# First keys of a sequence taken inside the last feed-forward turns, and two blocks of scores moved ahead of key tiles 3 and 4

## The chip, the cores and the metric

The kernel runs on one NeuronCore of a Trainium2 chip. Its engines are TensorE (PE, matrix products), VectorE (DVE), ScalarE (ACT), GpSimd (POOL) and SyncE (SP, which issues the transfers here). They run side by side and meet at semaphores. The metric is device time in microseconds (us): the median of several runs.

## The reference

The input x is 2 sequences of 4096 rows of 256 numbers. Three layers follow each other: a feed-forward layer, a causal attention, and the same feed-forward layer again.

```
x = x + 0.5 * ffn(layernorm(x))          # mix over 3 rows, 9 paths, argmax picks one, layernorm
x = x + attention(layernorm(x))
x = x + 0.5 * ffn(layernorm(x))

# attention(x):
q, k, v = x @ Wq.T + bq, x @ Wk.T + bk, x @ Wv.T + bv
scores  = q @ k.T / 16
masked  = where(causal, scores * sign(scores), -inf)    # the absolute value of the score
out     = softmax(masked) @ v
return out @ Wo.T + bo
```

## The kernel before, in words

**Tiles.** A tile is 512 rows (4 blocks of 128). There are 16 tiles, 8 per sequence. All products run in three fp16 matmuls (high x high, high x low, low x high), so most data exist as a high part, made by ACT, and a low part, made by DVE.

**Feed-forward (`ffn(0)`, `ffn(1)`).** Each engine goes through turns -6 to 16, and in turn t works on several tiles at different stages. At the end of a tile stand `result` (DVE adds the path's product to the row, and counts `y_done`), `squares` (ACT), `result_scale` (POOL, the reciprocal root), `result_scaled` and `result_added` (DVE), and a store by SP, which counts `stored`. The product of tile 15 goes to its own PSUM banks 6 and 7. While turns 11 to 15 run, the first five tiles of x1 (the result of the first layer) are loaded back, and DVE and POOL work out their means and deviations (`first_stats`, `first_scales`).

**Attention (`attention(b)`, b = 0 and 1).** W_q and W_k are folded into one matrix and W_v and W_o into another, so the normalised rows serve as keys and as values. For each key tile t:
- `key_rows(t)` (ACT or DVE) normalises the rows in place,
- `keys(t, c)` (PE) transposes them into two PSUM banks,
- `keyT_high` (ACT) and `keyT_low` (DVE; `key_lows` is both halves) make the fp16 parts of the transposed keys,
- `key_high` (ACT) and `key_low` (POOL) make those of the rows as values.

`query(j, c)` (PE) makes the queries of tile j, `q_high` (ACT) and `q_low` (DVE) their parts. `group((j, m))` is a block of scores of query tile j against key tile m: PE makes four strips, ACT takes the absolute value (`absolute`) and DVE the running maximum (`score_max`). Key tiles 0 to 4 and the blocks (0, 0) and (1, 0) are made before the steps; then `step(j)`, j = 0 to 7, does the rest. A step opens with a transpose of the running maximum (PE, L1878), a reduce on DVE (L1139) and a transpose back (PE, L1887), from which ACT makes `max_row`. DVE subtracts it from the scores (L1041), ACT takes the exponential and its high part (L1458, L1462), DVE the low part (L1047), and PE multiplies with the values.

**What sets the order.** Nothing schedules this program: every engine runs its instructions in the order in which its block is written, and waits where the code says so. Waits that matter here: before sequence 0 PE waits for `y_done` of all 16 tiles; `keys_wait(t)` on PE waits for the low part of key tile t; `query(j, c)` and the first block of scores of a query tile wait for `spare_free[c]`, which `q_low` and the two users of banks 6 and 7 at a step's opening count; a block of scores waits until ACT has emptied the same strip of the block before it (`abs_done`); POOL's `key_low` before sequence 0 waits for `x1_done` of all 16 tiles; SP loads key tile 5 when all 16 tiles are stored. Between the sequences, key tiles 0 to 2 and queries 0 and 1 of the next sequence are made inside step 7 of the one before; key tiles 3 and 4 are made after it, together with the four outputs of the last tile.

Of the kernel before, what the change touches and what calls it, by code (L numbers as in the profile page):

```python
# [49 lines left out]
def macaron(nc, x, Wq, bq, Wk, bk, Wv, bv, Wo, bo, mix, W1, b1, W2, b2, Wo1, bo1, Wo2, bo2,  # L50
# [11 lines left out]
    with ctx:  # L62
# [208 lines left out]
        def key_bank(t):  # L271
            return 4 if t % 2 == 0 else 0
# [60 lines left out]
        def use(ph, t):  # L333

            return ph * NTT + t
# [35 lines left out]
        def out_banks(t):  # L371

            return ps_n if t == NTT - 1 else ps_o

# [295 lines left out]
        def _(dve):  # L670
# [140 lines left out]

            def ffn(ph):
# [33 lines left out]

                def result_scaled(t):

                    dve.wait_ge(r_rstd, use(ph, t) + 1)
                    for u in range(SUB):  # L850
                        at = cols(n_rows(t), u * D, D)
                        ins = v.scalar_tensor_tensor(out=at, in0=at, scalar=y_rstd[:, u:u + 1], in1=gamma_b[:, :],  # L852
                                                     op0=ALU.mult, op1=ALU.mult)
                    ins.then_inc(scaled_done, 1)

                def result_added(t):

                    dve.wait_ge(xb_done, use(ph, t) + 1)
                    dve.wait_ge(scaled_done, use(ph, t) + 1)
                    v.tensor_tensor(n_rows(t), n_rows(t), x_rows(t), ALU.add).then_inc(x1_done, 1)  # L860
# [52 lines left out]
                def turn(t):  # L913
# [45 lines left out]
                    if last:  # L959
                        result_scaled(t - 1)  # L960
# [4 lines left out]
                    if last:  # L965
                        result_added(t - 1)
                        if ph == 0 and 0 <= t - 1 - NT < EARLY:
                            added_sums(t - 1)
# [8 lines left out]
            def attention(b):  # L977
# [225 lines left out]
                if b == 0:  # L1203
                    for t in range(EARLY - 1):
                        key_lows(t)
                        if t in (1, 2):
                            for c in range(DC):
                                q_low(t - 1, c)
                        if t < 2:
                            key_rows(EARLY - 2 + t)  # L1210
                    group(one_by_one(0, 0, True), None, lambda i: None)
                    key_lows(EARLY - 1)
                else:
# [5 lines left out]
                    output(s_last, 1)  # L1219
                    for c in range(DC):  # L1220
                        keyT_low(AHEAD_KEYS, c, LATE_BANK)
                    score_max(*maxima[2])
                    output(s_last, 2)
                    score_max(*maxima[3])
                    output(s_last, 3)
                    key_rows(AHEAD_KEYS + 1)
# [19 lines left out]
        def _(act):  # L1246
# [42 lines left out]

            def ffn(ph):  # L1290
# [27 lines left out]

                def squares(t):
                    g = use(ph, t)  # L1320
                    act.wait_ge(y_done, g + 1)
                    if g >= 1:
                        act.wait_ge(r_eps, g)
                    for u in range(SUB):
                        ins = a.activation(cols(square, u * D, D), cols(n_rows(t), u * D, D), ACT.Square, accum_out=y_sq[:, u:u + 1])  # L1325
                    ins.then_inc(sq_done, 1)
# [37 lines left out]
                def turn(t):  # L1364
# [9 lines left out]
                    if last:  # L1374
                        squares(t - 1)
# [19 lines left out]
            def attention(b):  # L1395
# [172 lines left out]
                if b == 0:  # L1568
                    key_rows(0)
                    keysT_high(0)  # L1570
                    key_rows(1)
                    keysT_high(1)
                    key_rows(2)

                    act.wait_ge(stored, 16 * (NTT - 2))
                    for j in range(2):
                        for c in range(DC):
                            q_high(j, c)
                        keysT_high(j + 2)
                        key_high(j)  # L1580
                    group(None, (0, 0, True), None, lambda i: None)
                    absolute(SUB - 1, True, blocks(act, b, 0, 0), ring_at(act, 0, 0))
                    keysT_high(EARLY - 1)
                    for t in range(2, EARLY):
                        key_high(t)
# [429 lines left out]
```

## Time and profile before

| | |
|---|---|
| runs | 1462.21, 1463.25, 1463.43 us, median 1463.25 |
| profiled execution, from first to last instruction | 1460.0 us |
| PE busy | 1336.2 us (92%) |
| DVE busy | 1178.4 us (81%) |
| ACT busy | 923.2 us (63%) |
| POOL busy | 326.0 us (22%) |
| mean granted clock of TensorE | 0.977 |

The profiled execution is told by its span alone; the median of the runs is 3.25 us above it. `ffn(0)` fills the first 320 us, sequence 0 goes to about 750 us, sequence 1 to about 1190 us, and `ffn(1)` fills the rest. A busy share is a mean over all of these; the change touches two short stretches, the passage from `ffn(0)` to sequence 0 (about 300 to 350 us) and the one from sequence 0 to sequence 1 (about 750 to 785 us), and those have to be looked at by themselves.

### The profile page before, as it was taken

The numbers are of one execution on the slowest core, as the hardware profiler recorded it, in microseconds if no ns is written. First come the engines' busy times: TensorE is split into PE (matmuls) and PEld (weight loads), VectorE is DVE, ScalarE is ACT, GpSimd is POOL, SyncE is SP. The second block draws the span as 40 slices with busy tenths as digits, with TensorE's granted clock in tenths as the row PEclk, the third lists the DMA queues.
The fourth block names the chain that finished last, engine by engine and source line by source line (L and its number), as shares of the span: only waits on it lengthen the run. The fifth ranks groups of instructions, "written<-read, shape, count | busy, mean of one in ns | idle before, by whom it ended". The sixth has DMA issues, their size and how long they took to land.

```text
span 1460.0 us, 24657 instructions
## 1 busy us (share of the span) xinstructions
PE 1336.2 (92%) x7700; PEld 773.8 (53%) x7700; DVE 1178.4 (81%) x2326; ACT 923.2 (63%) x1717; POOL 326.0 (22%) x359
## 2 busy tenths in 40 slices
PE   3999998868999999999879999999998879999995
PEld 2567765644454454544344455454544336777764
DVE  5999998876778777788875787787778768989986
ACT  5676764446567666566866567666575866766641
POOL 2255553432010000040011010000130004555422
PEclk9899999979999999999999999999999989999998
DMA  6243333320001100011201010000002211433321
GB/s 157 51 125 109 113 99 91 92 73 0 16 29 36 38 0 29 1 44 38 79 1 44 30 44 16 29 15 15 29 15 74 86 32 51 121 93 108 92 79 58
DMA packets 86985, 82.18 MB, mean 56 GB/s; under 512 B 8539, under 2 KB 86884, under 8 KB 86884
## 3 DMA queue, kind: packets, MB, share of 16 engines
q1 hardware_dynamic: 86884, 80.91, 18.4%
q8 instruction: 54, 0.88, 0.3%
q14 instruction: 47, 0.39, 0.1%
HBM read 55.43 MB, written 25.46 MB: 55 GB/s over the span
## 4 chain that ended last, share of the span: by engine, by line
PE 64%; DVE 15%; issue 9%; ACT 8%; POOL 2%; DMA 1%; DVEq 0%; ACTq 0%; POOLq 0%; SPq 0%
PE PS L1618 57%; DVE R L1047 2%; PE PS L1626 2%; DVE R L1041 2%; PE PS L1716 2%; ACT R L1458 2%; ACT R L1462 2%; DVE run_max L1035 1%; PE PS L1687 1%; DVE x_st L1069 1%; ACT R L1417 1%; POOL R L608 1%; DVE R L852 1%; DVE st L751 1%; DMA R<-in_L_attn_x 1%
## 5 line engine op out<-in xcount | busy, mean ns | idle before, releaser
L1618 PE MATMUL PS<-R 128*128 128x512 f16 (+3 forms) x3456 | 718.4, 362 | 36.1 <-DVE R L1047 29.7
L1618 PEld LDWEIGHTS PS<-R 128*128 128x128 f16 (+1 forms) x3456 | 325.9, 98 | 395.6 <-DVE R L1047 58.8
L1047 DVE TENSOR_TENSOR R<-R 128x512 f16<-128x512 f32 (+3 forms) x288 | 188.7, 655 | 96.1 <-ACT R L1462 94.4
L1449 ACT ACTIVATE R<-PS 128x512 f32 (+5 forms) x288 | 160.3, 558 | 158.8 <-PE PS L1618 158.8
L1458 ACT ACTIVATE R<-R 128x512 f32<-128x512 f32 (+4 forms) x288 | 169.6, 589 | 52.2 <-DVE R L1041 51.3
L1618 PE MATMUL PS<-R,w_hi 128*128 128x512 f16 x640 | 195.5, 388 | 4.3 <-DVE R L801 4.3
L1618 PE MATMUL PS<-w_hi,R 128*128 128x256 f16 x1024 | 189.0, 274 | 10.5 <-DVE R L843 10.5
L1462 ACT ACTIVATE R<-R 128x512 f16<-128x512 f32 (+3 forms) x288 | 171.1, 594 | 26.7 <-ACT R L1458 0.4
L1041 DVE TENSOR_TENSOR R<-R,max_row 128x512 f32<-128x512 f32 (+4 forms) x288 | 186.8, 648 | 0.5 <-ACT max_row L1526 0.5
L1035 DVE TENSOR_TENSOR run_max<-run_max,R 128x512 f32<-128x512 f32 (+3 forms) x272 | 175.6, 645 | 8.4 <-DVE run_max L1035 1.7
L575 POOL TENSOR_SCALAR veps<-mv 128x4 f32<-128x4 f32 x48 | 16.4, 343 | 653.4 <-issue 376.0
L1618 PE MATMUL PS<-w_lo,R 128*128 128x256 f16 x512 | 140.2, 274 | 0.0
L904 DVE SCALAR_TENSOR_TENSOR R<-PS,b1c,R 128x512 f32<-128x512 f32 x128 | 93.4, 742 | 38.3 <-PE PS L1618 37.5
L1618 PE MATMUL PS<-R,w_lo 128*128 128x512 f16 x320 | 123.8, 387 | 0.0
L1618 PEld LDWEIGHTS PS<-w_hi,R 128*128 128x128 f16 x1024 | 100.6, 98 | 37.6 <-DVE R L843 13.4
L640 POOL TENSOR_TENSOR R<-R 128x1024 f16<-128x1024 f32 x16 | 34.2, 2154 | 308.6 <-ACT R L1424 308.6
L1626 PE MATMUL PS<-ident,R 128*128 128x128 f32 x384 | 58.6, 298 | 39.7 <-ACT R L1266 18.8
L1325 ACT ACTIVATE R<-R 128x256 bf16<-128x256 f32 x128 | 51.6, 404 | 61.9 <-DVE R L843 61.9
L1618 PEld LDWEIGHTS PS<-R,w_hi 128*128 128x128 f16 x640 | 60.9, 103 | 52.3 <-issue 4.7
L910 DVE TENSOR_TENSOR R<-R 128x1024 f16<-128x1024 f32 x64 | 77.7, 1214 | 0.0
L1272 ACT ACTIVATE R<-PS 128x1024 f32<-128x1024 f32 x32 | 32.8, 1025 | 69.6 <-PE PS L1626 69.5
L608 POOL TENSOR_TENSOR R<-R,beta_b 128x1024 f32<-128x1024 f32 x32 | 75.3, 2354 | 4.9 <-DVE R L901 4.7
(124 smaller groups left out, 1752.5 us busy)
## 6 DMA issues: line engine op xcount, KB each, us to landing
R<-x_scratch SPq DMA_DIRECT2D x48, 512.0 KB, 4.1
x_scratch<-R SPq DMA_DIRECT2D x32, 512.0 KB, 3.2
R<-oh_scratch SPq DMA_DIRECT2D x32, 320.0 KB
R<-in_L_attn_x SPq DMA_DIRECT2D x16, 512.0 KB, 5.1
R<-oh_scratch SPq DMA_DIRECT2D x32, 256.0 KB
out<-R SPq DMA_DIRECT2D x16, 512.0 KB, 3.2
R<-in_L_ffn_W SPq DMA_DIRECT2D x2, 288.0 KB
R<-in_L_ffn_W SPq DMA_DIRECT2D x1, 512.0 KB
```

The costliest lines, as they stand in the source:

```text
L608: g.tensor_tensor(rows4(x_rows(t)), rows4(x_rows(t)), beta_b[:, :].unsqueeze(1).to_broadcast([P, SUB, D]), ALU.add).then_inc(xb_done, 1)
L904: v.scalar_tensor_tensor(out=at, in0=ps_h[:, h_bank[g, c], :], scalar=b1c[:, c:c + 1], in1=chunk(mask, t, c), op0=ALU.add, op1=ALU.mult).t ...
L910: v.tensor_tensor(chunk(hlo, t, c, n), masked_chunk(t, c, n), chunk(hhi, t, c, n), ALU.subtract)\
L1035: v.tensor_tensor(run_max[:, lo:], run_max[:, lo:], cols(ring, at, TT - lo), ALU.max)\
L1041: v.tensor_tensor(cols(ring, at, TT - lo), cols(ring, at, TT - lo), max_row[:, lo:], ALU.subtract)\
L1047: v.tensor_tensor(p_lo[:, i * TT + lo:(i + 1) * TT], pf[:, (i % 2) * TT + lo:(i % 2 + 1) * TT], p_hi[:, i * TT + lo:(i + 1) * TT], ALU.sub ...
L1325: ins = a.activation(cols(square, u * D, D), cols(n_rows(t), u * D, D), ACT.Square, accum_out=y_sq[:, u:u + 1])
L1449: a.activation(cols(ring, ring_m + i * TT + lo, TT - lo), ps_s[:, i, lo:], ACT.Abs, scale=1.0 / (QS * XS * D ** 0.5)).then_inc(abs_done, 1)
L1458: a.activation(p, cols(ring, ring_n + i * TT + lo, TT - lo), ACT.Exp)\
L1462: a.activation(p_hi[:, i * TT + lo:(i + 1) * TT], p, ACT.Copy).then_inc(phi_done, 1)
L1618: ins = t_.matmul(dst, w, xx, start=start and n == 0, stop=stop and n == last, skip_group_check=skip)
L1626: ins = t_.transpose(dst[:, u * P:(u + 1) * P], cols(rows, u * D + c * P, P), ident[:, :])
```

## The change

Passage 1, `ffn(0)` to sequence 0:
- PE waits for `y_done` of 15 tiles only, transposes key tiles 0 and 1, and then waits for tile 15. Key tile 1 goes to banks 0 and 1, the others to banks 4 and 5. Block (0, 0) follows query 1 at once and no longer waits for key tile 2's low part; block (1, 0) stands between key tiles 3 and 4.
- ACT normalises key tiles 0 and 1 inside turn 15 and key tile 2 after the high parts of 0 and 1. `squares` of tile 15 moves behind the high part of key tile 2.
- DVE does `result_scaled` and `result_added` of tiles 14 and 15 between the low parts, and the maxima of block (0, 0) before the low part of key tile 3.

Passage 2, sequence 0 to sequence 1: block (1, 0) stands before key tiles 3 and 4 on PE, with outputs 2 and 3 inside it; ACT and DVE follow.

```diff
         def key_bank(t):
-            return 4 if t % 2 == 0 else 0
+            return 0 if t == 1 else 4
...
+        def left_over(ph, t):
+
+            return ph == 0 and t >= NTT - 2
...
-                    if last:
-                        result_scaled(t - 1)
+                    if last and not left_over(ph, t - 1):
+                        result_scaled(ph, t - 1)
```

On DVE, before sequence 0:

```diff
                 if b == 0:
-                    for t in range(EARLY - 1):
-                        key_lows(t)
-                        if t in (1, 2):
-                            for c in range(DC):
-                                q_low(t - 1, c)
-                        if t < 2:
-                            key_rows(EARLY - 2 + t)
+                    key_lows(0)
+                    key_lows(1)
+                    result_scaled(0, NTT - 2)
+                    for c in range(DC):
+                        q_low(0, c)
+                    key_lows(2)
+                    key_rows(3)
+                    result_added(0, NTT - 2)
+                    for c in range(DC):
+                        q_low(1, c)
+                    key_rows(4)
+                    result_scaled(0, NTT - 1)
                     group(one_by_one(0, 0, True), None, lambda i: None)
-                    key_lows(EARLY - 1)
+                    result_added(0, NTT - 1)
+                    key_lows(3)
+                    key_lows(4)
```

On ACT, in the turn:

```diff
+                    if ph == 0 and t == NTT - 1:
+                        first_key_rows(0)
+                        first_key_rows(1)
```

On PE, before sequence 0 and, under `else`, before sequence 1:

```diff
                 if b == 0:
-                    pe.wait_ge(y_done, NTT)
-                    for t in range(EARLY - 1):
...
+                    pe.wait_ge(y_done, NTT - 1)
+                    for t in range(2):
                         for c in range(DC):
                             keys(t, c, key_bank(t))
...
+                    pe.wait_ge(y_done, NTT)
...
                 else:
+                    def late_outputs(i):
+                        if i == 1:
+                            for u in range(2, SUB):
+                                output(b * NT - 1, b * SPARE + 2, u)
+
                     keys_wait(AHEAD_KEYS - 1)
                     group((0, 0, True), None, lambda i: None)
                     for u in range(2):
                         output(b * NT - 1, b * SPARE + 2, u)
+                    group((1, 0, False), None, late_outputs)
                     for c in range(DC):
                         keys(AHEAD_KEYS, c, LATE_BANK)
-                    for u in range(2, SUB):
-                        output(b * NT - 1, b * SPARE + 2, u)
                     keys_wait(AHEAD_KEYS)
                     for c in range(DC):
                         keys(AHEAD_KEYS + 1, c, LATE_BANK)
-                group((1, 0, False), None, lambda i: None)
```

The order of PE's instructions at the end of passage 1, before: the rows are key tile 3 (transposes), block (0, 0) in four rows, key tile 4, block (1, 0) and the opening of step 0.

```order
L1626 MATMUL PS<-ident,R 128x128 x8
L1618 MATMUL PS<-R 128x512 x6
L1618 MATMUL PS<-R 128x384 x6
L1618 MATMUL PS<-R 128x256 x6
L1618 MATMUL PS<-R 128x128 x6
L1626 MATMUL PS<-ident,R 128x128 x8
L1618 MATMUL PS<-R 128x512 x24
L1878 MATMUL PS<-ident,run_max 128x128 x4
```

And now, PE at the same place of the changed kernel, from block (0, 0) on:

```order
L1641 MATMUL PS<-R 128x512 x6
L1641 MATMUL PS<-R 128x384 x6
L1641 MATMUL PS<-R 128x256 x6
L1641 MATMUL PS<-R 128x128 x6
L1649 MATMUL PS<-ident,R 128x128 x8
L1641 MATMUL PS<-R 128x512 x24
L1649 MATMUL PS<-ident,R 128x128 x8
L1901 MATMUL PS<-ident,run_max 128x128 x4
```

Block (0, 0) stands ahead of key tile 3 and block (1, 0) ahead of key tile 4, whose transposes are now the last thing before step 0.

DVE in passage 1, before, from `result` of tile 14 (L843) on; L852 is `result_scaled`, L860 `result_added`, L1007 a low part of keys, L995 `key_rows`.

```order
L843 SCALAR_TENSOR_TENSOR R<-PS,R 128x1024
L751 BN_STATS st<-R 128x6 x4
L758 BN_AGGR mv<-st 128x2 x4
L852 SCALAR_TENSOR_TENSOR R<-R,y_rstd,gamma_b 128x256 x4
L860 TENSOR_TENSOR R<-R 128x1024
L843 SCALAR_TENSOR_TENSOR R<-PS,R 128x1024
L852 SCALAR_TENSOR_TENSOR R<-R,y_rstd,gamma_b 128x256 x4
L860 TENSOR_TENSOR R<-R 128x1024
L1007 TENSOR_TENSOR R<-PS,R 128x512 x2
L995 TENSOR_SCALAR R<-R,key_rstd,key_shift 128x256 x4
```

And now, DVE from `result` of tile 14 (L862) on; L821 is `result_scaled`, L829 `result_added`, L1011 a low part of keys, L1022 one of a query, L999 `key_rows`.

```order
L862 SCALAR_TENSOR_TENSOR R<-PS,R 128x1024
L755 BN_STATS st<-R 128x6 x4
L762 BN_AGGR mv<-st 128x2 x4
L862 SCALAR_TENSOR_TENSOR R<-PS,R 128x1024
L1011 TENSOR_TENSOR R<-PS,R 128x512 x4
L821 SCALAR_TENSOR_TENSOR R<-R,y_rstd,gamma_b 128x256 x4
L1022 SCALAR_TENSOR_TENSOR R<-PS,R 128x512 x2
L1011 TENSOR_TENSOR R<-PS,R 128x512 x2
L999 TENSOR_SCALAR R<-R,key_rstd,key_shift 128x256 x4
L829 TENSOR_TENSOR R<-R 128x1024
L1022 SCALAR_TENSOR_TENSOR R<-PS,R 128x512 x2
```

`result` of tile 15 follows that of tile 14 with only the statistics between them, and the scaling and adding of both tiles comes later, between the key and query parts.

PE in passage 2, before: the last output row, key tile 4, block (1, 0) and the opening of step 0.

```order
L1618 MATMUL PS<-wvo_lo,R 128x257
L1618 MATMUL PS<-wvo_hi,R 128x257
L1626 MATMUL PS<-ident,R 128x128 x8
L1618 MATMUL PS<-R 128x512 x24
L1878 MATMUL PS<-ident,run_max 128x128 x4
```

And now, PE at the same place: outputs 2 and 3 end in the first two rows, the second half of block (1, 0) follows, then key tiles 3 and 4.

```order
L1641 MATMUL PS<-wvo_lo,R 128x257
L1641 MATMUL PS<-wvo_hi,R 128x257
L1641 MATMUL PS<-R 128x512 x12
L1649 MATMUL PS<-ident,R 128x128 x16
L1901 MATMUL PS<-ident,run_max 128x128 x4
```

No product is added or dropped on PE; the two key tiles moved behind the block of scores.

## Rows read from the trace of the kernel before

**Rows 1.** Waits of PE, whole span: who waited, for whom, us, times, longest

```profile
PE PS L1626 <- ACT R L1417: 13.6, 2, 10.9
PE PS L1626 <- DVE R L995: 6.2, 1, 6.2
```

**Rows 2.** Windows, passage 1: busy time of each engine, granted clock, DMA

```profile
305.00:310.00 5.00, 0.00 (x0) 0.00 (x0) 4.60 (x5) 0.00 (x0) 4.65 (x6) 0.85 0.00 0
310.00:315.00 5.00, 0.00 (x0) 0.00 (x0) 1.84 (x3) 3.45 (x12) 2.04 (x5) 0.50 0.31 105
```

**Rows 3.** Timeline of PE, passage 1: start, us, instruction, idle before it and releaser

```profile
315.37 1.94 PE L1626 MATMUL PS<-ident,R 128*128 128x128 f32 x8 [10.89 <-ACT R L1417]
...
327.10 0.59 PE L1618 MATMUL PS<-R,wqk_hi 128*128 128x512 f16 x2
...
329.69 1.04 PE L1626 MATMUL PS<-ident,R 128*128 128x128 f32 x8
332.68 3.43 PE L1618 MATMUL PS<-R 128*128 128x512 f16 x24 [1.95 <-DVE R L1007]
335.95 1.04 PE L1626 MATMUL PS<-ident,R 128*128 128x128 f32 x8
336.83 5.34 PE L1618 MATMUL PS<-R 128*128 128x512 f16 x24
342.01 0.60 PE L1878 MATMUL PS<-ident,run_max 128*128 128x128 f32 x4
```

**Rows 4.** Timeline of DVE, passage 1

```profile
300.92 1.22 DVE L843 SCALAR_TENSOR_TENSOR R<-PS,R 128x1024 f32<-128x1024 f32 x1
...
314.68 1.67 DVE L852 SCALAR_TENSOR_TENSOR R<-R,y_rstd,gamma_b 128x256 f32<-128x256 f32 x4 [3.16 <-POOL y_rstd L598]
316.46 1.22 DVE L860 TENSOR_TENSOR R<-R 128x1024 f32<-128x1024 f32 x1
...
334.82 0.29 DVE L1028 TENSOR_TENSOR R<-R,tri 128x128 f32<-128x128 f32 x1 [2.19 <-ACT R L1449]
...
337.68 1.28 DVE L1007 TENSOR_TENSOR R<-PS,R 128x512 f16<-128x512 f32 x2
...
343.25 2.03 DVE L1032 COPY run_max<-R 128x512 f32<-128x512 f32 x1
...
350.17 0.68 DVE L1041 TENSOR_TENSOR R<-R,max_row 128x512 f32<-128x512 f32 x1
```

**Rows 5.** Timeline of ACT, passage 1

```profile
313.16 2.06 ACT L1417 ACTIVATE R<-R,key_shift,key_rstd 128x256 f32<-128x256 f32 x4
...
336.59 1.09 ACT L1430 ACTIVATE R<-PS 128x512 f16<-128x512 f32 x2 [0.16 <-PE PS L1626]
337.56 2.95 ACT L1424 ACTIVATE R<-R 128x1024 f16<-128x1024 f32 x3
```

**Rows 6.** Timeline of POOL, passages 1 and 2

```profile
338.70 6.30 POOL L640 TENSOR_TENSOR R<-R 128x1024 f16<-128x1024 f32 x3 [4.09 <-ACT R L1424]
...
756.45 4.25 POOL L640 TENSOR_TENSOR R<-R 128x1024 f16<-128x1024 f32 x2 [115.82 <-ACT R L1424]
```

**Rows 7.** Timeline of PE, passage 2

```profile
764.13 1.94 PE L1626 MATMUL PS<-ident,R 128*128 128x128 f32 x8 [6.25 <-DVE R L995]
765.87 7.03 PE L1618 MATMUL PS<-R 128*128 128x512 f16 x24
...
774.46 0.60 PE L1887 MATMUL PS<-ident,max_col 128*128 128x128 f32 x4
```

**Rows 8.** Timeline of DVE, passage 2

```profile
758.09 0.64 DVE L1028 TENSOR_TENSOR R<-R,tri 128x128 f32<-128x128 f32 x1
758.76 2.23 DVE L1035 TENSOR_TENSOR run_max<-run_max,R 128x256 f32<-128x256 f32 x1
...
767.35 1.39 DVE L1069 BATCH_NORM_STATS2 x_st<-R 128x6 f32<-128x256 f32 x4
...
780.89 0.68 DVE L1041 TENSOR_TENSOR R<-R,max_row 128x512 f32<-128x512 f32 x1
```

More of the change, by code:

```diff
@@ L810, in set_beginnings, with result_scaled, result_added @@
                 v.memset(chunk(mask, 1, 0)[0:DM, :], 0.0).then_inc(edges_set, 1)
+            def result_scaled(ph, t):
+                dve.wait_ge(r_rstd, use(ph, t) + 1)
+                for u in range(SUB):
+                    at = cols(n_rows(t), u * D, D)
+                    ins = v.scalar_tensor_tensor(out=at, in0=at, scalar=y_rstd[:, u:u + 1], in1=gamma_b[:, :],
+                                                 op0=ALU.mult, op1=ALU.mult)
+                ins.then_inc(scaled_done, 1)
+            def result_added(ph, t):
+                dve.wait_ge(xb_done, use(ph, t) + 1)
+                dve.wait_ge(scaled_done, use(ph, t) + 1)
+                v.tensor_tensor(n_rows(t), n_rows(t), x_rows(t), ALU.add).then_inc(x1_done, 1)
             def ffn(ph):
@@ L845, in result @@
                         .then_inc(y_done, 1)
[L847 to L860, printed above, removed]
                 def added_sums(t):
@@ L964, in turn @@
                             masked_low(t + HIDDEN, 2)
-                    if last:
-                        result_added(t - 1)
+                    if last and not left_over(ph, t - 1):
+                        result_added(ph, t - 1)
                         if ph == 0 and 0 <= t - 1 - NT < EARLY:
@@ L1219, in attention @@
                     output(s_last, 1)
+                    score_max(*maxima[2])
+                    score_max(*maxima[3])
+                    key_rows(AHEAD_KEYS + 1)
+                    output(s_last, 2)
+                    output(s_last, 3)
                     for c in range(DC):
                         keyT_low(AHEAD_KEYS, c, LATE_BANK)
[L1222 to L1226, printed above, removed]
                     for c in range(DC):
@@ L1288, in x_high, with squares, first_key_rows @@
                 a.activation(cols(xhi, g % XBUF * DC * TT, DC * TT), xm, ACT.Copy).then_inc(xhi_done, 1)
+            def squares(ph, t):
+                g = use(ph, t)
+                act.wait_ge(y_done, g + 1)
+                if g >= 1:
+                    act.wait_ge(r_eps, g)
+                for u in range(SUB):
+                    ins = a.activation(cols(square, u * D, D), cols(n_rows(t), u * D, D), ACT.Square, accum_out=y_sq[:, u:u + 1])
+                ins.then_inc(sq_done, 1)
+            def first_key_rows(t):
+                act.wait_ge(f_scaled, t + 1)
+                act.wait_ge(f_in[t], 16)
+                for u in range(SUB):
+                    at = cols(rows_in[t], u * D, D)
+                    ins = a.activation(at, at, ACT.Identity, bias=key_shift[:, t, u:u + 1], scale=key_rstd[:, t, u:u + 1])
+                ins.then_inc(a_rows[t], 1)
             def ffn(ph):
@@ L1373, in turn @@
                         middle(ph, t + MIX)
-                    if last:
-                        squares(t - 1)
+                    if ph == 0 and t == NTT - 1:
+                        first_key_rows(0)
+                        first_key_rows(1)
+                    if last and not (ph == 0 and t == NTT):
+                        squares(ph, t - 1)
                     if rows_on(ph, t + ROWS):
@@ L1592, in attention @@
                     key_high(0)
+                    group(None, (1, 0, False), None, lambda i: None)
                     keysT_late(AHEAD_KEYS)
@@ L1595, in attention @@
                     keysT_late(AHEAD_KEYS + 1)
-                    for t in range(2, EARLY):
-                        key_high(t)
-                group(None, (1, 0, False), None, lambda i: None)
+                for t in range(2, EARLY):
+                    key_high(t)
                 over_steps(act, step)
```

58 lines of the change are left out of this document (28 added, 30 removed).

## The prediction, made before the changed kernel was run

> **What bounds the kernel now.** I read the waits of PE first, because PE is busy 92% of the span and everything else hides behind it. Two of its waits belong to the passages that the change touches: 13.6 us for ACT's L1417, in two pieces, and 6.2 us for DVE's L995 in one [rows 1]. Then I read the windows of passage 1. Between 305 and 315 us PE does nothing, and the granted clock falls to 0.50, which is 1.2 GHz; it is back at 2.4 GHz only when PE has worked again for some us [rows 2]. Last come the timelines, engine by engine, to see who holds whom. In passage 1 PE stands idle for 10.9 us before it transposes key tile 0 at 315.37, so it ended tile 15's product at about 304.5 [rows 3]. It waits because ACT normalises the rows of key tile 0 only at 313.16 [rows 5], after `squares` of tile 15, which waits for DVE's `result` of tile 15, which stands on DVE behind the scaling of tile 14. In passage 2 PE waits 6.25 us for the rows of key tile 4, and the block of scores that follows it takes 7.03 us for the work that took 5.2 in passage 1 [rows 7, 3], because the clock fell in that gap.
>
> **Passage 1, step by step.** Prices of PE's pieces at 2.4 GHz, as distances between starts in [rows 3]: a key tile 336.83 - 335.95 = 0.9, a pair of queries 329.69 - 327.10 = 2.6, block (0, 0) 335.95 - 332.68 = 3.3, block (1, 0) 342.01 - 336.83 = 5.2 us. From the start of a key tile to the end of its second low part I build 2.4 us: 0.65 until ACT starts on the first half (336.59 - 335.95, [rows 3, 5]), 1.1 for ACT's two copies [rows 5], 0.6 for the last low part, and small gaps.
>
> *Front.* ACT is free from about 294 and normalises key tiles 0 and 1 there, 2 x 2.06 us [rows 5]; nothing waits behind them but `squares` of tile 14, whose input comes at 302.1 (300.92 + 1.22, [rows 4]). Cost nothing, cover 4 us. PE then goes from tile 15's product (304.4) straight into key tiles 0 and 1, until 306.1. DVE makes `result` of tile 15 at 304.5 to 305.7, key lows 0 at 305.7 to 306.9 and 1 until 308.2 (0.6 us each, two in 1.28 in [rows 4]). PE: queries 0 at 306.95 to 309.55 (waiting 0.85), key tile 2 to 310.4, queries 1 to 313.05, block (0, 0) to 316.35, key tile 3 to 317.25, block (1, 0) to 322.45. ACT has 2.06 us of key rows 2 in between and is done with them at 309.2, in time.
>
> *DVE becomes the longer queue.* After key lows 1 (308.2) it runs: scaling of 14, 1.65 (start 314.68, [rows 4]), query lows 0, 1.2 (to 311.0), key lows 2, 1.2 (to 312.2), key rows 3, 1.35, adding of 14, 1.15 (start 316.46, [rows 4]), query lows 1, 1.2 (to 316.0), key rows 4, 1.35, scaling of 15, 1.65, the maxima of (0, 0), 337.68 - 334.82 = 2.9, adding of 15, 1.15 (to 323.0), key lows 3, 1.2: 324.2. The price of key rows is that of four 128x256 operations at 0.33; no row shown has it, and the four scalings bound it from above with 1.65. PE waits for key lows 3 from 322.45 to 324.3, makes key tile 4 until 325.2 and opens step 0 (L1878) there instead of at 342.01: 16.8 us earlier. DVE must still make key lows 4 (to 326.8) and the reduce (to 327.4), so the transpose back starts at 327.4. Before it came 1.7 us after L1878, at 343.7: **16.3 us earlier**. The clock never falls here, since PE's gaps are 0.85 and 1.85 us, where before the mean of 0.85 in the window from 305 puts the fall at about 308.5, after 4 us without work [rows 2].
>
> *What is late next.* `x1_done` of 16 tiles now comes at 323.0, so POOL makes its five `key_low` of 2.1 us each (6.30 for three, [rows 6]) from 323.0 until 333.6 or later (ACT's last three high parts, 2.95 us from 326.05 [rows 5], are in time for it). Before, they ended at 345.0, that is 3.0 us after L1878; now 8.4 us after it. They matter for what they take from DVE, not for what they make. The copy of the first maximum at 343.25 took 2.03 us because it ended only with POOL's last operation, and in passage 2 a small operation took 0.64 us and the next, 128x256, 2.23 us beside two of POOL's [rows 4, 6, 8]: the two take turns, one operation each. DVE's operations that read PSUM ran beside POOL undelayed. After the reduce DVE has a copy and three maxima to make from SBUF, and each lets one `key_low` through: POOL's work of 10.6 us from 323.0 plus three such turns of 0.45 ends at about 335.0, the last maximum at 335.2. Then come the two query lows (1.2) and L1041 at **336.4**; it stood at 350.17. That is 13.8 us, against 16.3 with no such delay; I take 13.7. The whole chain behind L1041 (exponential, high part, low part, values on PE) keeps its length. The bounds are 16.3 (POOL yields, or runs ahead) and 11.5 (every DVE operation here takes the 2.23 us of [rows 8]: 5 x 2.23 from 327.4 ends 3 us later than I have it, less 0.8 of overlap).
>
> [...]
>
> *The store and the loads behind it.* Tile 15 is stored some 5 us later than before, at about 326, and SP's loads of key tile 5 and of the first residual stand behind it, landing at about 331. DVE looks at tile 5 in a later step, tens of us on. Cost nothing.
>
> **Passage 2, step by step** (times as in the before trace, as if passage 1 had changed nothing). PE ends outputs 0 and 1 at 754.4. Then block (1, 0) with outputs 2 and 3 inside it, 5.2 + 1.3, to 760.85, key tile 3 to 761.75; its rows are ready, and those of tile 4 come at 759.6 at the latest, delayed by one `key_low`. ACT and DVE make the parts of key tile 3 until 763.3 (2.4 from the start of its transposes), PE key tile 4 at 763.35 to 764.2 and L1878 there. On DVE key lows 4 end at 765.75, then the four sums of the outputs, 1.39 us [rows 8], which were hidden before, end at 767.1, and the reduce at 767.8. The transpose back starts at 767.8 instead of 774.46 [rows 7]: **6.65 us earlier**. POOL's second `key_low` now waits for ACT's high part 1 (763.5), so three and a half of them lie beside the copy and the maxima; by the same turns the last maximum ends at 773.8 and L1041 starts at 775.0 instead of 780.89 [rows 8]: **5.9 us**. Bounds: 8.7, which is what L1878 gains (765.87 + 7.03 = 772.9 against 764.2, [rows 7]) if the sums cost nothing, and 3.5, if each of the DVE operations takes 2.23.
>
> **The sum.** 13.7 + 5.9 = 19.6 us of the profiled 1460.0, which is 1440.4. The median of the runs stood 3.25 above the profiled span, so the runs give **1443.7**. Nothing between the passages changes in work, and PE is the bound there, so the gain is carried to the end.
>
> **The rivals.**
> - *POOL costs nothing.* Its operations fall beside PSUM reads of DVE, or DVE is served first. For it: the order of arrivals is close. Against: [rows 8]. 16.3 + 6.65 = 22.95: 1440.3 us. Chance 0.2.
> - *The clock falls in the new gap.* While DVE is held up, PE has no work from about 332.4 to 336.4, 4.0 us; the same length of idleness brought the clock down before [rows 2, 3]. Then some 7 us run at 1.2 GHz, as the block of [rows 7] did, of which PE was working about half or more: 3.4 us lost. Against: the gap is only just that long. 16.2 gained: 1447 us. Chance 0.15.
> - *Only passage 1 pays, or DVE's queue is longer than summed.* In passage 2 DVE gets the sums and POOL at once and gives back what PE won: 13.7 gained, 1449.5 us. Much the same comes out if three of DVE's operations in passage 1 are stretched by POOL as in [rows 8], 1.8 us each, with none of it hidden. Chance 0.12.
> - *It does not do what it says.* PE still waits for tile 15 or for rows in place of its neighbours, and passage 1 gains only the 10.9 us of idleness less the new waits, about 8 us: 1455. Chance 0.03.
> - *Slower.* The clock falls before 310 us, since PE has several short waits there, and stays at 1.2 GHz through both passages. PE's work from 304.4 to L1878 is 5 x 0.9 + 2 x 2.6 + 3.3 + 5.2 = 18.2 us, at half the clock 36.4, ending at 341: gain 1 us. In passage 2, 9.6 us of work take 19.2 and end where they ended before: gain 0. With 3 us more lost in each following step the time is 1468. For it: [rows 2] show the clock low through such a passage. Against: it rose there as soon as PE worked without a break. It decides only if the clock is low for more than 30 us. Chance 0.03.
>
> **How the numbers follow.** The forecast has 0.47, with its own range of 1441.5 to 1446. With the rivals on either side, 1439 to 1450.5 leaves out the last two, the far end of the third and what lies below 1439: 2 in 10. A change within 0.2% (3 us) cannot be told from none in this kernel: faster by more than that needs under 1460.3, and only the slower rival and a little of the one before it miss this. Faster 0.94, same 0.03, slower 0.03.
>
> **What the profile will show.** If the steps are right: PE's first transposes of keys within 1 us of tile 15's product, at clock 1.00; no PE wait for key rows over 1 us in either passage; L1901 (the old L1878) at about 325; a PE wait for DVE's key lows 3 of 1 to 2 us; a copy or maximum on DVE of over 2 us between 327 and 336 beside POOL's `key_low`; in passage 2, a PE wait before L1910 of 1 to 2 us for DVE's reduce. The forecast is wrong if the clock is below 1.00 anywhere between 305 and 345, if the first L1045 of step 0 starts far from 336, or if a later step has a PE wait that was not there before.

## The result and the profile after

| | before | after |
|---|---|---|
| median of the runs | 1462.73 us (4 runs, 1461.53 to 1463.43) | 1444.58 us (4 runs, 1444.09 to 1445.54) |
| span of the profiled execution | 1460.0 us | 1442.5 us |
| PE busy | 1336.2 us | 1335.2 us |

The ratio is 0.9881, with a 95% interval of 0.987 to 0.9893. The forecast was 1443.7 us. PE works as long as before; what went is idleness and low clock in the two passages.

Where the gain is made can be read exactly, because each step opens with the same two PE instructions in both traces. The table takes the differences of their starts, and those of the first subtraction behind them (L1041 before, L1045 now), each against the same start ahead of the passage (`result` of tile 14 for passage 1, the first subtraction of step 7 for passage 2). The last column, the first subtraction of step 1, is the gain that is left one step later:

| gain in us at | opening of step 0 | transpose back | first subtraction | first subtraction of step 1 |
|---|---|---|---|---|
| passage 1, forecast | 16.8 | 16.3 | 13.7 | 13.7 |
| passage 1, measured | 17.06 | 16.45 | 13.75 | 13.57 |
| passage 2, forecast | 8.7 | 6.65 | 5.9 | 5.9 |
| passage 2, measured | 8.39 | 6.48 | 5.29 | 4.63 |

PE's timeline in passage 1 of the changed kernel (start, us, instruction, idle before it and releaser) answers to [rows 3]:

```profile
303.74 1.91 PE L1649 MATMUL PS<-ident,R 128*128 128x128 f32 x16
306.62 0.59 PE L1641 MATMUL PS<-R,wqk_hi 128*128 128x512 f16 x2 [0.97 <-DVE R L1011]
...
312.67 3.42 PE L1641 MATMUL PS<-R 128*128 128x512 f16 x24
315.93 1.04 PE L1649 MATMUL PS<-ident,R 128*128 128x128 f32 x8
316.80 5.34 PE L1641 MATMUL PS<-R 128*128 128x512 f16 x24
323.45 1.09 PE L1649 MATMUL PS<-ident,R 128*128 128x128 f32 x8 [1.31 <-DVE R L1011]
324.38 0.60 PE L1901 MATMUL PS<-ident,run_max 128*128 128x128 f32 x4
...
326.72 0.65 PE L1910 MATMUL PS<-ident,max_col 128*128 128x128 f32 x4 [0.44 <-DVE max_col L1143]
...
336.03 9.23 PE L1641 MATMUL PS<-R 128*128 128x512 f16 x39 [4.11 <-DVE R L1022]
```

The gap of 10.9 us is gone: 16 transposes follow tile 15's product without a pause. PE waits 0.97 us and 1.31 us for low parts of keys, as the forecast had it (0.85 and 1.85). Before, block (0, 0) waited 1.95 us for the low part of key tile 3 (at 332.68, [rows 3]); now it stands ahead of that tile and the wait is gone. The new and largest wait is the last one, 4.11 us for the query's low part.

DVE's timeline tells why; before, the copy took 2.03 us and the subtraction stood at 350.17 [rows 4]:

```profile
325.98 0.68 DVE L1143 TENSOR_REDUCE max_col<-PS 128x4 f32<-128x512 f32 x1
326.58 2.30 DVE L1036 COPY run_max<-R 128x512 f32<-128x512 f32 x1
328.98 5.75 DVE L1039 TENSOR_TENSOR run_max<-run_max,R 128x512 f32<-128x512 f32 x3
334.65 1.28 DVE L1022 SCALAR_TENSOR_TENSOR R<-PS,R 128x512 f16<-128x512 f32 x2
335.85 0.68 DVE L1045 TENSOR_TENSOR R<-R,max_row 128x512 f32<-128x512 f32 x1
```

POOL at that time, where it ended at 345.0 before [rows 6]:

```profile
322.28 11.11 POOL L644 TENSOR_TENSOR R<-R 128x1024 f16<-128x1024 f32 x5 [7.04 <-DVE R L829]
```

The copy and three maxima take 8.2 us, where pool_late, below, has 2.8 us for them without POOL beside them. POOL's five `key_low` run through the same time and are stretched too, from 10.6 to 11.1 us.

Windows of passage 1 after (busy time of PE, PEld, DVE, ACT, POOL, then the granted clock), where [rows 2] had a dead PE and a clock of 0.50 from 308.5 on:

```profile
330.00:335.00 5.00, 1.92 (x14) 0.84 (x12) 4.79 (x4) 1.47 (x3) 3.39 (x2) 1.00 0.00 0
335.00:340.00 5.00, 3.96 (x11) 1.25 (x12) 4.85 (x11) 2.92 (x7) 0.00 (x0) 0.66 0.00 0
```

The 17 us at 1.2 GHz are gone, but a new stretch of 3.4 us at that level begins at 335.7, at the end of the gap of 4.11 us.

Passage 2, PE and DVE after, against [rows 7, 8]:

```profile
749.34 1.09 PE L1649 MATMUL PS<-ident,R 128*128 128x128 f32 x8 [1.57 <-DVE R L1011]
750.27 0.60 PE L1901 MATMUL PS<-ident,run_max 128*128 128x128 f32 x4
...
753.91 0.65 PE L1910 MATMUL PS<-ident,max_col 128*128 128x128 f32 x4 [1.75 <-DVE max_col L1143]
...
761.72 2.09 PE L1641 MATMUL PS<-R 128*128 128x512 f16 x6 [2.60 <-DVE R L1022]
```

```profile
742.23 3.18 DVE L999 TENSOR_SCALAR R<-R,key_rstd,key_shift 128x256 f32<-128x256 f32 x4
...
751.87 1.40 DVE L1073 BATCH_NORM_STATS2 x_st<-R 128x6 f32<-128x256 f32 x4
753.19 0.67 DVE L1143 TENSOR_REDUCE max_col<-PS 128x4 f32<-128x512 f32 x1
753.78 0.78 DVE L1036 COPY run_max<-R 128x512 f32<-128x512 f32 x1
754.66 5.76 DVE L1039 TENSOR_TENSOR run_max<-run_max,R 128x512 f32<-128x512 f32 x3
```

The wait of 6.25 us for the rows of key tile 4 is gone. DVE normalises these rows (L999) earlier, in 3.18 us for four, one of them held beside a `key_low`. The sums of the outputs (L1073) and the reduce hold the transpose back for 1.75 us, and the maxima are stretched here as well. Behind the gap of 2.60 us the six matmuls take 2.09 us where they take 1.46 at the full clock.

### The profile page after: what moved, and what is told of

Read it like the earlier page. It is cut to its first block, busy times and chain, and to the rows that moved or that the text cites. A ratio compares the mean times of both kernels' runs of the same rounds, so it can differ in the third digit from the quotient of the medians.

```text
span 1442.5 us, 24659 instructions
## 1 busy us (share of the span) xinstructions
PE 1335.2 (93%) x7700; PEld 772.8 (54%) x7700; DVE 1181.9 (82%) x2326; ACT 922.6 (64%) x1717; POOL 328.1 (23%) x359
## 4 chain that ended last, share of the span: by engine, by line
PE 62%; DVE 17%; issue 9%; ACT 7%; POOL 2%; DMA 1%; DVEq 0%; ACTq 0%; POOLq 0%; SPq 0%
PE PS L1641 56%; DVE R L1051 2%; DVE R L1045 2%; PE PS L1739 2%; PE PS L1649 2%; DVE run_max L1039 2%; ACT R L1481 2%; ACT R L1485 1%; DVE x_st L1073 1%; PE PS L1710 1%; DMA R<-in_L_attn_x 1%; DVE R L821 1%; POOL R L612 1%; DVE R L908 1%; ACT R L1440 1%
## 5 line engine op out<-in xcount | busy, mean ns | idle before, releaser
L1641 PE MATMUL PS<-w_hi,R 128*128 128x256 f16 x1024 | 188.2, 273 | 10.9 <-DVE R L862 10.9
L1039 DVE TENSOR_TENSOR run_max<-run_max,R 128x512 f32<-128x512 f32 (+3 forms) x272 | 180.8, 665 | 8.4 <-DVE run_max L1039 1.7
L1045 DVE TENSOR_TENSOR R<-R,max_row 128x512 f32<-128x512 f32 (+4 forms) x288 | 186.9, 649 | 0.5 <-ACT max_row L1549 0.5
```

What stands on the lines that cost most here:

```text
L1039: v.tensor_tensor(run_max[:, lo:], run_max[:, lo:], cols(ring, at, TT - lo), ALU.max)\
L1045: v.tensor_tensor(cols(ring, at, TT - lo), cols(ring, at, TT - lo), max_row[:, lo:], ALU.subtract)\
L1641: ins = t_.matmul(dst, w, xx, start=start and n == 0, stop=stop and n == last, skip_group_check=skip)
```

## The experiments

Theory: the front of passage 1 and the score order of passage 2 make independent gains, and part of both is lost because POOL's `key_low` and VectorE's copy and maxima take turns. Rivals: the gain is all of one passage; POOL has nothing to do with the late subtraction; the order of scores makes the gain in passage 1 too. All gains below are read as in the table above, from one profile each; "back" is the transpose back, "kept" the gain at the first subtraction of step 1. Ahead of passage 1, where the edits change nothing that PE waits for, the profiled executions already stand from 1.8 us later to 1.25 us earlier than the one before, so a median tells less than these columns. Medians are of 4 or 5 runs (11 for p2_only), ratios against the kernel before on the same chip.

| kernel | median us | ratio (95%) | passage 1: back, subtraction, kept | passage 2: back, subtraction, kept |
|---|---|---|---|---|
| after_again | 1445.36 | 0.989 (0.9873, 0.9906) | 16.45, 13.76, 13.50 | 6.48, 5.28, 2.90 |
| p1_only | 1449.79 | 0.9911 (0.9897, 0.9924) | 16.46, 13.77, 13.53 | -0.24, -0.24, -0.23 |
| p2_only | 1458.72 | 0.9977 (0.9968, 0.9986) | -0.05, -0.05, -0.05 | 6.48, 5.29, 4.80 |
| pool_late | 1444.75 | 0.9874 (0.9859, 0.9889) | 16.46, 16.41, 15.26 | 6.49, 6.44, 5.29 |
| pool_memset | 1441.24 | 0.9852 (0.9837, 0.9867) | 16.46, 16.41, 16.41 | 6.48, 6.44, 6.44 |
| p1_tail_old | 1448.36 | 0.9903 (0.9888, 0.9918) | 17.24, 14.98, 12.07 | 6.48, 5.29, 5.29 |
| sums_late | 1448.24 | 0.9901 (0.9885, 0.9916) | 16.45, 13.75, 13.74 | 7.76, 3.96, 2.38 |
| pool_slots | 1441.9 | 0.9859 (0.9844, 0.9875) | 16.45, 16.40, 16.05 | 6.44, 6.39, 6.05 |
| slots_sums | 1440.44 | 0.985 (0.9837, 0.9864) | 16.45, 16.39, 16.05 | 7.76, 7.71, 7.36 |
| slots_sums_tail | 1441.66 | 0.9861 (0.9845, 0.9877) | 17.25, 17.24, 15.42 | 7.78, 7.73, 7.38 |

**p1_only.** The edit puts the old order back before sequence 1, on PE (and accordingly on DVE and ACT):

```diff
                     for u in range(2):
                         output(b * NT - 1, b * SPARE + 2, u)
-                    group((1, 0, False), None, late_outputs)
                     for c in range(DC):
                         keys(AHEAD_KEYS, c, LATE_BANK)
...
+                    group((1, 0, False), None, lambda i: None)
```

> Passage 1 as in the changed kernel, passage 2 as before. My theory: the two gains are independent, and passage 1 brings 16 us until the transpose back of step 0 and 13.5 to 14 us at the first L1045 behind it, because GpSimd's key_low operations hold VectorE's copy and maxima there; 13.5 us stay until passage 2, and the median is 1448.5 to 1450. Rival 1 (passage 1 is worth little by itself, the keys of passage 2 make up the rest): over 1452. Rival 2 (passage 2's new order costs in truth): under 1446.

1449.79 us, as the theory said. Passage 1's gain is the same to 0.04 us with and without passage 2's.

**p2_only.** The kernel before, with passage 2 changed:

```diff
                     for u in range(2):
                         output(b * NT - 1, b * SPARE + 2, u)
+                    group((1, 0, False), None, late_outputs)
```

> Passage 1 as before, passage 2 as in the changed kernel. My theory: 4.6 to 5.5 us faster than before, 1457 to 1458: 8.4 us at the opening of step 0 of sequence 1, 6.5 at the transpose back (the four sums of the outputs and the reduce stand in its way), 5.3 at the first L1045. Rival (the order of scores is worth the whole of PE's wait of 6.25 us and the low clock behind it): 8 us or more, under 1455.

The steps are the expected ones (8.4, 6.5, 5.3), but the median of 1458.72 is 0.7 us above the upper edge of what I expected, a gain of 3.65 us in place of 4.6 or more; the interval of the ratio reaches from 2.0 to 4.7 us. In its profile 1.1 us are lost at the passage to the last layer, which has nothing to do with the edit (below). The rival's 8 us are excluded.

**pool_late.** POOL is held back:

```diff
                 for t in range(EARLY):
+                    if t == 2:
+                        pool.wait_ge(max_done, b * BLOCKS + 3 * SUB)
                     key_low(t)
```

> The changed kernel, with GpSimd's key_low of tiles 2, 3 and 4 held back until the maxima of block (1, 1) are made. My theory, that GpSimd and VectorE take turns at operations from SBUF: VectorE's copy takes 0.4 us and three maxima 2.0 us instead of 2.3 and 5.75, the first L1045 comes 2.5 us earlier in passage 1 and 1.1 in passage 2, PE's gap of 4.1 us shrinks to 1.5, the clock no longer falls behind either passage (0.2 to 0.7 us each): 3 to 5 us faster than the changed kernel, 1439.5 to 1441.5. If the collisions only move into step 0's low parts, up to 2 us less of it each. Rival (PE waits there for ScalarE's query parts, and GpSimd has nothing to do with it): no change within 0.5 us.

The steps are the expected ones, the median is not. The copy and the maxima are short again, and so the subtraction comes only 0.05 us later than the transpose back allows, in place of 2.7 and 1.2 us. DVE in passage 1 of pool_late:

```profile
328.69 0.42 DVE L1038 COPY run_max<-R 128x512 f32<-128x512 f32 x1
329.21 2.28 DVE L1041 TENSOR_TENSOR run_max<-run_max,R 128x512 f32<-128x512 f32 x3
...
342.24 1.59 DVE L1053 TENSOR_TENSOR R<-R 128x128 f16<-128x128 f32 x1 [0.76 <-ACT R L1487]
...
346.62 1.57 DVE L1038 COPY run_max<-R 128x512 f32<-128x512 f32 x1
```

But 1.15 us of it are given back in each passage, where the three `key_low` meet the copy of step 1 (1.57 us). The low part of 1.59 us costs nothing: PE has work. PE's gap is 1.46 us and the clock does not fall behind either passage. But the median of 1444.75 is no better than the changed kernel's and so on the rival's number; what speaks against the rival is the subtraction, 2.66 and 1.15 us earlier than in the changed kernel. The profiled execution lost 2.3 us at the passage to the last layer and 1.6 ahead of passage 1 against the one before, places that the edit does not touch.

**pool_memset.** Three of POOL's five operations only write; the low parts of key tiles 2 to 4 as values are left out:

```diff
+                    if 2 <= t < EARLY:
+                        g.memset(cols(KV_lo, t * SUB * D, SUB * D), 0.0).then_inc(a_lo, 1)
+                        return
                     g.tensor_tensor(cols(KV_lo, t * SUB * D, SUB * D), rows_in[t], cols(KV_hi, t * SUB * D, SUB * D),
                                     ALU.subtract).then_inc(a_lo, 1)
```

> The changed kernel, with GpSimd's key_low of tiles 2, 3 and 4 replaced by a memset of the same cells, which leaves out the low parts of those values: GpSimd writes SBUF and reads nothing. My theory by the rule that only a read of GpSimd holds VectorE's two-input operations: the three maxima take 0.6 to 0.7 us each whatever the memsets take, and the gain is that of pool_late without moved collisions, 3.5 to 5 us, 1439.5 to 1441. The copy may still be held, since it has one input only and was held before. Rival 1 (any operation of GpSimd holds VectorE): the maxima are stretched by the length of a memset each. Rival 2 (GpSimd has nothing to do with it): no change.

1441.24 us; 16.41 and 6.44 us are kept whole. In passage 2 the maxima, of which the first lies wholly beside the third memset, take 2.28 us for three as when they are alone; the copy of passage 1 is held for the length of all three memsets. DVE and POOL in passage 1, then in passage 2:

```profile
328.14 2.87 DVE L1039 COPY run_max<-R 128x512 f32<-128x512 f32 x1
331.11 2.28 DVE L1042 TENSOR_TENSOR run_max<-run_max,R 128x512 f32<-128x512 f32 x3
```

```profile
327.99 2.73 POOL L645 MEMSET R<- 128x1024 f16 x3
...
750.83 3.06 POOL L645 MEMSET R<- 128x1024 f16 x3 [0.52 <-ACT R L1450]
```

The third of these memsets by itself:

```profile
752.72 1.18 POOL L645 MEMSET R<- 128x1024 f16 x1
```

```profile
752.48 0.52 DVE L1039 COPY run_max<-R 128x512 f32<-128x512 f32 x1
753.11 2.28 DVE L1042 TENSOR_TENSOR run_max<-run_max,R 128x512 f32<-128x512 f32 x3
```

So rival 2 is out, and rival 1 is out for the maxima, though on one overlap only: the first of them runs from 753.11 to 753.80, inside the memset of 752.72 to 753.90. The theory's price of POOL is settled: 2.7 us in passage 1 and 1.2 in passage 2 at the subtraction. The copy is the exception: even operations that only write hold it in passage 1. In passage 2 it took 0.52 us across the end of the second memset, and the third, which started under it, took 1.18 us where the others take 0.95.

**p1_tail_old.** The old order of scores with the new front (on PE; DVE makes the low part of key tile 3 before the scaling of tile 15, and ACT follows):

```diff
-                    group((0, 0, True), None, lambda i: None)
                     keys_wait(2)
                     for c in range(DC):
                         keys(3, c, key_bank(3))
-                    group((1, 0, False), None, lambda i: None)
+                    group((0, 0, True), None, lambda i: None)
                     keys_wait(3)
                     for c in range(DC):
                         keys(4, c, key_bank(4))
+                    group((1, 0, False), None, lambda i: None)
```

> The changed kernel, but in passage 1 the blocks of scores stand in the old order: key tile 3 before block (0, 0), key tile 4 before block (1, 0), low parts of key tile 3 before the scaling of tile 15. My theory: in passage 1 the front (keys 0 and 1 at once, late scaling and adding) makes nearly all of the gain, and the order of scores is worth under 1 us: the transpose back of step 0 within 1 us of the changed kernel's, the first L1045 0.5 to 1.5 us later since the last adding, and with it GpSimd's work, comes 1.2 us later; the median within 1.5 us of the changed kernel's. Rival (a block of scores hides a whole wait for the parts of a key tile): 3 us or more slower than the changed kernel.

The transpose back comes 0.8 us earlier, not later, than with the new order, and the subtraction 1.2 us earlier: my theory had the sign of the second wrong, because the shorter queue on DVE before the reduce outweighs POOL's later start. Of the 16.5 us none is thus due to the order of scores. But only 12.07 us are kept. Windows of passage 1 in this kernel:

```profile
335.00:340.00 5.00, 3.26 (x9) 0.99 (x8) 4.82 (x13) 3.68 (x8) 0.00 (x0) 0.52 0.00 0
340.00:345.00 5.00, 5.00 (x22) 2.33 (x21) 1.17 (x5) 1.22 (x4) 0.00 (x0) 0.79 0.00 0
```

The clock is at 1.2 GHz for 6.8 us from 335.2, where the changed kernel has 3.4. DVE, POOL and PE show a second cause of the 2.9 us that go between the subtraction and the next step:

```profile
334.01 1.41 DVE L1045 TENSOR_TENSOR R<-R,max_row 128x512 f32<-128x512 f32 x1
```

```profile
322.86 12.00 POOL L644 TENSOR_TENSOR R<-R 128x1024 f16<-128x1024 f32 x5 [8.25 <-DVE R L829]
```

```profile
337.64 9.49 PE L1641 MATMUL PS<-R 128*128 128x512 f16 x42 [1.74 <-DVE R L1051]
346.97 0.61 PE L1901 MATMUL PS<-ident,run_max 128*128 128x128 f32 x4
```

The subtraction meets POOL's last `key_low`, which ends at 334.86, and takes 1.41 us in place of 0.68: PE starts on the values 3.63 us after the subtraction's start instead of 2.91 (353.08 - 350.17 before). From there to the opening of step 1 it needs 9.33 us in place of 7.15. So 0.7 us are the collision and 2.2 the low clock; neither theory had them. The median of 1448.36 is 3.8 us above the first one of the changed kernel, which is the number of the rival; its mechanism is refuted by the transpose back, which lost nothing. The profiled execution took 1445.81 us, inside the expected range, and the other three 1448.33 to 1448.43: what these lost besides is not shown.

**sums_late.** The sums of the last output leave the place ahead of the reduce:

```diff
                         if is_int(j, 0) and i == SUB:
+                            if b:
+                                for u in range(SUB):
+                                    output_sums(s_last, u, xr)
...
-                    for u in range(SUB):
-                        output_sums(s_last, u, xr)
```

> The changed kernel, with the four sums of the last output moved behind the maxima of block (1, 0) in passage 2. My theory: the reduce and the transpose back come 1.3 us earlier in passage 2, but GpSimd's turns with the copy and the maxima end when they did, and the sums then stand before the query parts: the first L1045 of sequence 1 comes at most 0.3 us earlier, or up to 1.4 later. Median within 1.5 us of the changed kernel's. Rival (the transpose back sets the end): 1.3 us faster.

The steps are as expected: the transpose back gains 1.3 us, the subtraction loses 1.3, since the maxima take 5.76 us as before and the sums come on top. PE's gap grows to 5.21 us, the clock falls for 6.8 us, and the median is worse than I allowed for: its four runs (1447.49 to 1448.55) all lie above the eight of the changed kernel (1444.09 to 1446.39). This is the trap in a plain form: PE's visible wait before L1910 was not the one that set the end.

**pool_slots.** POOL's work placed in VectorE's idle time:

```diff
                 for t in range(EARLY):
+                    if t in (2, 4):
+                        pool.wait_ge(max_done, b * BLOCKS + (2 if t == 2 else 3) * SUB)
                     key_low(t)
```

> The changed kernel, with GpSimd's key_low of tiles 2 and 3 held back until the maxima of block (1, 0) are made, and that of tile 4 until those of block (1, 1). They then lie beside VectorE's idle time and its reads of PSUM. My theory: the 2.65 us at the first L1045 of passage 1 that pool_late won are kept but for some 0.4, and the copy of step 1, which pool_late stretched from 0.4 to 1.6 us, is short again: 3.5 to 4.5 us faster than the changed kernel, 1440 to 1441. Rival (each key_low costs VectorE the same wherever it stands): as pool_late, within 1 us of the changed kernel.

1441.9 us, 0.9 above the upper edge of what I expected. The subtraction is held by 0.3 us only (L1047, the subtraction here, takes 1.02 in place of 0.68), and 16.05 and 6.05 us are kept. The clock does not fall behind either passage. The rival is out: what a `key_low` costs depends on what it meets.

**slots_sums.** Both edits. 

> pool_slots and sums_late together. My theory: with GpSimd out of the way the sums fill VectorE's idle time between the maxima and the query parts, and the transpose back sets the time of passage 2: 1 to 1.3 us faster than pool_slots, 1439 to 1440. Rival (the sums are on no path in either): no change against pool_slots within 0.3 us.

1440.44 us, 0.4 above the expected range; 1.3 us more in passage 2, as expected, by the very edit that alone brought the subtraction 1.3 us later than in the changed kernel. It has the lowest median of the study.

**slots_sums_tail.** The same with the old order of scores in passage 1. 

> slots_sums with the tail of p1_tail_old: the old order of scores and key tiles in passage 1. My theory: the old order opened step 0 earlier (transpose back 17.24 us gained against 16.45) and lost it again only because GpSimd's work was later and PE's gap brought the clock down; with key_low of tiles 2 to 4 held back it keeps 16.6 to 17 us of passage 1, 0.6 to 0.9 us more than slots_sums: 1439.5 to 1440. Rival (the new order of scores is itself what keeps passage 1's gain): 1 us or more slower than slots_sums, over 1441.5.

The median is 1.2 us above slots_sums and so on the number that I had given the rival, but the two were not run on the same chip, and their runs overlap (1440.17 to 1442.27 against 1439.6 to 1441.21). My theory failed in one step, and the trace gives another cause than the rival's. 17.24 us are there at the subtraction's start, but 15.42 are kept. DVE and POOL in passage 1:

```profile
333.46 2.50 DVE L1047 TENSOR_TENSOR R<-R,max_row 128x512 f32<-128x512 f32 x1
```

```profile
324.58 4.41 POOL L644 TENSOR_TENSOR R<-R 128x1024 f16<-128x1024 f32 x2 [8.24 <-DVE R L831]
331.21 4.21 POOL L644 TENSOR_TENSOR R<-R 128x1024 f16<-128x1024 f32 x2 [2.22 <-DVE run_max L1041]
```

With the opening earlier, the subtraction falls into the second of the two `key_low` and takes 2.50 us. The shift of 0.8 us turned a collision of 0.3 us into one of 1.8; the passages together keep 22.8 us against 23.4 in slots_sums. Another 1.6 us of its profile went at the passage to the last layer. Whether the old order with a better place for that `key_low` would win was not tried.

**after_again.** 

> The changed kernel once more, beside slots_sums_tail on one chip, so that the two can be compared: 1444 to 1445.5. Its profile shows how much of the loss at the passage to the last layer (1.2 us in the first profile) is of the kernel: if it comes from where the clock falls, it differs between executions of one kernel.

1445.36 us. The steps repeat to 0.1 us up to the subtractions of step 0. What differs is the clock: in passage 2 it is low for 6.8 us in place of 3.4, and 2.90 us are kept in place of 4.63; at the passage to the last layer it is low for 10.2 us in place of 13.7, and nothing is lost against the one before, which has 10.2 us there too, in place of 1.2. Passage 2 stands in two other profiles with the same gain at the subtraction (5.29): p2_only, low for 3.4 us, kept 4.80, and p1_tail_old, where the clock stayed at 1.00 behind the same gap of 2.60 us, kept all of it.

## Why the prediction was right

*Front of passage 1: right.* ACT's early key rows cost nothing, and all starts of PE up to step 0 are within 0.3 us of the working once the 0.6 us that this execution had gained earlier are taken off. p1_tail_old shows that this front, not the order of scores, makes the gain.

*DVE becomes the longer queue: right.* The sum of thirteen prices missed the end of the queue by less than 0.3 us. PE's wait for key lows 3 was 1.31 us, where 1.85 were forecast.

*What is late next: right, and the term that mattered.* A sum that stopped at the transpose back would have had 22.95 us, and the rival that said so is refuted by pool_late and pool_memset, which get just these times when POOL is out of the way. The turns were forecast to put the subtraction at 336.4; it came at 335.85, at the same distance from the front. The lower bounds of 11.5 and 3.5 us counted five operations of 2.23 us where the queue has a copy and three maxima; the runs came nowhere near them. The Trainium skill (SBUF — State Buffer, "Who interferes with whom") states that a VectorE instruction with two SBUF inputs contends with a GpSimd instruction that reads SBUF, and not with one that only writes it. The trace agrees: a maximum took 2.4 us beside `key_low` and 0.69 beside a memset. It also states that a copy can enter a mode that contends with GpSimd. The copies of 2.30 us beside `key_low` and of 2.87 us beside memsets agree, though no trace names the mode.

*Passage 2: mechanism right, size off by 0.6 us.* 5.9 forecast, 5.29 measured. The transpose back was missed by 0.17 us; the rest lies between the reduce and the subtraction, which took 8.3 us from start to start where I had 7.9.

*The clock: the step that was wrong.* I gave the forecast a clock that does not fall in the passages and a rival of 0.15 a clock that falls in the new gap. The prediction had named a clock below 1.00 between 305 and 345 as a sign against it, and there it was, from 335.7 on. It fell in both passages and in both profiles of the changed kernel. It cost 0.2 and 0.3 us in passage 1, far less than the rival's 3.4, and 0.7 and 2.4 in passage 2. In passage 1 PE is busy for most of the low stretch, with six matmuls whose starts are 0.43 us apart in place of 0.22:

```profile
335.70:339.10 3.40, 3.06 (x7) 0.85 (x8) 3.25 (x8) 2.29 (x6) 0.00 (x0) 0.51 0.00 0
```

What that costs PE, about 1.3 us, comes out of a wait of 1.26 us for the first probabilities, which the kernel before has behind these six and the changed one has not:

```profile
350.36 1.46 PE L1618 MATMUL PS<-R 128*128 128x512 f16 x6 [1.46 <-issue]
353.08 7.32 PE L1618 MATMUL PS<-R 128*128 128x512 f16 x42 [1.26 <-DVE R L1047]
```

The steep price comes only when the low stretch reaches into the products that follow, as for 6.8 us in after_again (9.54 us from them to the opening of step 1 in place of 7.15).

*The sum.* Spans: 17.5 us gained, 19.6 forecast. The 2.1 between them are 0.6 from the size of passage 2, 0.2 and 0.7 from the clock behind the two subtractions, 0.1 in sequence 0 and 1.2 at the last layer, less 0.6 gained before passage 1 began (and 0.05 at its subtraction). The median came within 0.9 us all the same because I added 3.25 us for what lies around the span: that figure compared one execution's span with the median of others. In the changed kernel's profiled execution it is 1444.34 - 1442.5 = 1.8. Two errors of opposite sign, 2.1 and 1.4, nearly met; that the median came so close is luck in part.

*The slower rival* is out: the clock was at 1.00 from tile 15's product to 335 us. [rows 2] end at 315 and do not show when the clock came back in the kernel before; the windows behind them do. It was at 0.50 while PE worked almost without a break, and rose at 325.5:

```profile
320.00:325.00 5.00, 4.96 (x16) 2.88 (x17) 1.55 (x3) 3.52 (x7) 0.00 (x0) 0.50 0.62 209
325.00:330.00 5.00, 5.00 (x28) 2.87 (x27) 3.63 (x8) 3.35 (x7) 0.91 (x1) 0.95 0.05 14
```

## What to carry to other kernels

When a wait is removed, follow the chain past the first instruction that moves, to the first one that the next loop depends on, and ask on the way which engines now run side by side that did not before: here 3.9 us of 22.9 were lost to GpSimd's elementwise work standing beside VectorE's. A background operation should be placed against what it meets, by a wait on a semaphore that counts the other engine's critical work, and the placing must be looked at again after every shift, since 0.8 us earlier turned a collision of 0.3 us into one of 1.8. An edit that removes a visible wait and costs time alone may pay once the wait behind it is gone.

## What was not expected of the hardware

The same passage, with every start equal to 0.1 us, kept 4.63 or 2.90 us depending on whether the granted clock stayed at 1.2 GHz for 3.4 or for 6.8 us after a gap of 2.6 us; in p1_tail_old it did not fall behind that gap, and 5.29 were kept. At the passage to the last layer, which no edit touches, the kernels of this study lost, against the kernel before (10.2 us at the low clock), 0.0 us with 10.2 us at it, 1.1 to 1.6 with 13.7 and 2.3 to 2.5 with 17.1. So some 2 us of scatter between executions of these kernels go with the length of the low stretches; what decides that length is not shown. Closing the gaps of the two passages did not make the runs closer to each other: pool_slots, with no low stretch behind either passage, ran within 0.8 us from run to run, but slots_sums, also without one, within 1.6, and the changed kernel within 1.5 and, the second time, 2.1.

VectorE's copy from SBUF was held for 2.87 us by three memsets of GpSimd in a row in passage 1 of pool_memset, while a two-input operation of VectorE ran beside a memset in 0.69 us in passage 2. Beside `key_low`, which reads, both kinds were held, one operation per turn: the copy took 2.30 us in place of 0.42, a maximum 2.4 in place of 0.69.
